# A vision-transformer kernel: GpSimd's order at the end of the experts stage, and per-tile loads from two queues after it

## What is computed

```python
topk_logits, topk_idx = jax.lax.top_k(router_logits, TOP_K)          # 2 of 8 experts for each row
x_sort = x_flat[token_ids_sort]                                      # rows sorted by expert
gate, up = jnp.split(jax.lax.ragged_dot(x_sort, moe_w13, group_sizes), [MOE_DIM], axis=-1)
out_dispatch = jax.lax.ragged_dot(silu(gate) * up, moe_w2, group_sizes)
out_flat = zeros.at[token_ids_sort].add(out_dispatch * w_sort[:, None])
...
h = h + out_flat
h = h + _L1_attn_ref(_layernorm(h, axis=-1), ...)                    # second layer's attention
```

## Time and profile before

| | us |
|---|---|
| three runs | 1926.74, 1930.16, 1930.44 (median 1930.16) |
| the profiled execution | 1924.54 |
| its span, first to last instruction | 1922.8 |
| experts stage in the profile | 725.6 to 973.8 |
| next stage in the profile | 974.4 to 1026.4 |

### The profile page before, as it was taken

The page is one execution under the profiler, slowest core; times in us unless marked ns, Lnnn a source line. Parts: engine busy times, 40 slices in busy tenths (PEclk is TensorE's granted clock), DMA queues, the critical chain, the costliest instruction groups (busy, mean ns, idle before and its releaser), DMA issues. The chain is left out here.

```text
span 1922.8 us, 35451 instructions
## 1 busy us (share of the span) xinstructions
PE 1474.6 (77%) x10564; PEld 872.9 (45%) x10565; DVE 1430.1 (74%) x4678; ACT 856.9 (45%) x2116; POOL 614.7 (32%) x1114
## 2 busy tenths in 40 slices
PE   7799898978888857999963786676667777676664
PEld 4222224544444444666642444554445445554553
DVE  4688886567777683111146999999999999899982
ACT  2366665215555522222234544454545554554432
POOL 3300000350000012333301445554555554555540
PEclk9799999988999978999976667667677766766767
DMA  6351230241212250111045012101030012200000
GB/s 167 101 167 50 60 91 1 66 127 39 64 52 50 109 217 21 44 39 41 32 145 141 10 28 55 48 7 29 9 98 12 9 29 51 80 2 13 1 1 13
DMA packets 72136, 111.45 MB, mean 58 GB/s; under 512 B 8684, under 2 KB 57766, under 8 KB 71212
## 3 DMA queue, kind: packets, MB, share of 16 engines
q1 hardware_dynamic: 68236, 101.18, 18.3%
q0 software_dynamic: 3744, 8.42, 1.4%
HBM read 73.86 MB, written 37.52 MB: 58 GB/s over the span
## 5 line engine op out<-in xcount | busy, mean ns | idle before, releaser
L1679 DVE MATCH_REPLACE8 top_left<-top_next,top_left 128x65 f32<-128x65 f32 (+15 forms) x768 | 321.7, 426 | 0.0
L1674 DVE MAX8 top_next<-top_left 128x8 f32<-128x65 f32 (+15 forms) x768 | 300.3, 431 | 0.0
L1134 POOL TENSOR_TENSOR top_e<-top_e,top_left 128x33 f32<-128x33 f32 (+3 forms) x254 | 188.7, 765 | 199.8 <-DVE top_left L1679 199.6
L1409 ACT ACTIVATE top_e<-top_ps_s,top_neg_max 128x129 f32<-128x129 f32 (+15 forms) x256 | 125.8, 492 | 184.7 <-POOL top_neg_max L1578 168.5
L743 DVE TENSOR_REDUCE tok_rowmax<-tok_ps_s 128x1 f32<-128x512 f32 x256 | 166.8, 688 | 28.6 <-PE tok_ps_s L585 25.8
L1252 PE MATMUL top_ps_pt<-ident,top_e 128*128 128x128 f32 x640 | 140.3, 349 | 24.9 <-issue 13.6
L2530 DVE TENSOR_TENSOR moe_hid<-moe_act_gate,moe_ps_h 128x512 f32<-128x512 f32 x39 | 26.8, 688 | 163.9 <-ACT moe_act_gate L2491 163.9
L743 DVE TENSOR_REDUCE rot_rowmax<-rot_ps_s 128x1 f32<-128x128 f32 (+3 forms) x256 | 115.7, 487 | 43.4 <-PE rot_ps_s L588 39.6
L716 ACT ACTIVATE tok_et<-tok_ps_st 128x1024 f32<-128x1024 f32 x128 | 124.1, 1021 | 50.6 <-PE tok_ps_st L619 50.6
L2430 PE MATMUL moe_ps_h<-moe_w,moe_rows_t 128*128 x312 | 142.3, 599 | 0.2 <-issue 0.2
L1421 ACT ACTIVATE top_prob_t<-top_ps_pt 128x128 f32<-128x128 f32 (+3 forms) x256 | 104.9, 432 | 78.4 <-PE top_ps_pt L1252 77.7
(11 more groups left out here) (384 smaller groups left out, 3221.6 us busy)
## 6 DMA issues: line engine op xcount, KB each, us to landing
moe_w<-in_moe_w SPq DMA_DIRECT2D x3, 4096.0 KB, 22.0
last_xs<-zeros SPq DMA_DIRECT2D x1, 5120.0 KB, 20.1
moe_got<-moe_ys SPq DMA_DIRECT2D x8, 512.0 KB, 6.4
top_vs<-v_by_position SPq DMA_DIRECT2D x16, 256.0 KB
k_parts<-rot_parts SPq DMA_DIRECT2D x16, 192.4 KB, 3.2
rot_ks<-k_parts SPq DMA_DIRECT2D x16, 192.4 KB
top_ks<-k_parts SPq DMA_DIRECT2D x16, 192.4 KB
q_parts<-tok_parts SPq DMA_DIRECT2D x16, 192.0 KB, 2.9
```

The costliest lines, as they stand in the source:

```text
L1134: eng.tensor_tensor(e[:, U % KEPT, 0:w], e[:, U % KEPT, 0:w], left[:, U % 4, 0:w], ALU.subtract).then_inc(prob_ok, 1)
L1409: act.activation(e[:, U % KEPT, 0:keys(U)], row(U), ACT.Exp, bias=neg_max[:, U % 4:U % 4 + 1]).then_inc(e_ok, 1)
L1674: dve.max(next8[:, U % 2, step // 2, :], left[:, U % 4, 0:keys(U)]).then_inc(pick, 1)
L1679: ins = dve.match_replace(left[:, U % 4, 0:w], next8[:, U % 2, step // 2 - 1, :], left[:, U % 4, 0:w], 0.0)
```

## The change

In `run_gated_experts`, GpSimd's list keeps its order for tiles 0 to 31. It then scatters tile 31 at once, and goes through a nest: if tile j exists, gather tile j + 2, free the result buffer of tile j, scatter tile j, and ask for tile j + 1 inside; else wait for the last two scatters. In `combine_project`, the first image's results are loaded by tiles of 128 KB, choice 0 from SyncE's queue and choice 1 from GpSimd's, each tile with semaphores of its own; the other three images as before. ScalarE waits for `eps` and takes an unused square root before its masks.

```diff
             used = used_tiles(pool)
             lag = 3
-            for i in range(2, TILES + lag):
-                if i < SURE_TILES + 2:
-                    regather_rows(i)
-                    free_y(i - 2)
-                elif i < TILES + 2:
-                    with pool.If(used > i - 2):
-                        if i < TILES:
-                            regather_rows(i)
-                        free_y(i - 2)
-                j = i - lag
-                if 0 <= j < SURE_TILES:
+            for i in range(2, SURE_TILES + 2):
+                regather_rows(i)
+                free_y(i - 2)
+                if i >= lag:
+                    scatter_y(i - lag)
+            scatter_y(SURE_TILES - 1)
+
+            def rest(j):
+                if j == TILES:
+                    last_landed(j)
+                    return
+                with pool.If(used > j):
+                    if j + 2 < TILES:
+                        regather_rows(j + 2)
+                    free_y(j)
                     scatter_y(j)
-                elif j >= 0:
-                    with pool.If(used > j):
-                        scatter_y(j)
-            for j in range(SURE_TILES - 2, TILES):
-                if j < SURE_TILES:
+                    rest(j + 1)
+                with pool.Else():
+                    last_landed(j)
+
+            def last_landed(end):
+                for j in (end - 2, end - 1):
                     pool.wait_ge(y_sent[j % 2], 16 * (j // 2 + 1))
-                else:
-                    with pool.If(used > j):
-                        pool.wait_ge(y_sent[j % 2], 16 * (j // 2 + 1))
+
+            rest(SURE_TILES)
...
-            for b in range(B):
+            for n in range(NQ):
+                sp.dma_start(got[:, 0, n, :], ys[n * P:(n + 1) * P, :]).then_inc(got_in[1 + n], 16)
+            for b in range(1, B):
                 for k in range(2):
                     at = k * ROWS + b * S
                     sp.dma_start(got[:, k, b * NQ:(b + 1) * NQ, :], ys[at:at + S, :].rearrange("(n p) d -> p n d", p=P)
-                                 ).then_inc(got_in[b + 1], 16)
+                                 ).then_inc(got_in[NQ + b], 16)
...
+        @block.gpsimd
+        def _(pool):
+            for n in range(NQ):
+                at = ROWS + n * P
+                pool.dma_start(got[:, 1, n, :], c.ys[came][at:at + P, :]).then_inc(got_too[n], 16)
...
-                pe.wait_ge(got_in[0 if i == 0 else 1 + (i - 1) // NQ], 16 * 2)
+                if 1 <= i <= NQ:
+                    pe.wait_ge(got_in[i], 16)
+                    pe.wait_ge(got_too[i - 1], 16)
+                else:
+                    pe.wait_ge(got_in[0 if i == 0 else NQ + (i - 1) // NQ], 16 * 2)
...
-                if i == 0:
-                    act.wait_ge(eps_ok, 1)
...
+            act.wait_ge(eps_ok, 1)
+            act.activation(root[:, :], eps[:, :], ACT.Sqrt)
             mask_keys(0)
```

More of the change, by code:

```diff
@@ L2977, in combine_project @@
         eps = c.sbuf(st, "mixed_eps", [P, 1], F32)
+        root = c.sbuf(st, "mixed_root", [P, 1], F32)
         xn = c.ctx
@@ L2991, in combine_project @@
         ps_s = c.psum(st, "mixed_ps_sum", [P, 2, S])
-        got_in = [c.sem(st, f"{came}_got_in{i}") for i in range(B + 1)]
+        got_in = [c.sem(st, f"{came}_got_in{i}") for i in range(NQ + B)]
+        got_too = [c.sem(st, f"{came}_got_too{i}") for i in range(NQ)]
         sum_mm = c.sem(st, "mixed_sum_mm")
```

## The result

The changed kernel is slower. The median of its 18 fast runs is 1939.0 us against 1929.77 us for the kernel before (20 runs), and the ratio is 1.0048 with a 95% interval of 1.0035 to 1.0061; two further executions took 2930.77 and 6184.63 us, for a reason that isn't known, and are left out. That is 9.3 us more (6.8 to 11.8). The forecast was 7.6 more, 1937.8 in all.

What follows compares the result with a forecast made beforehand. TensorE's own list was taken to pace the experts stage and GpSimd's drain to set its barrier. +8.9 (gathers) + 0.4 (jumps) - 1.7 (loads) = +7.6 us, so 1937.8 us on the median; forecast 1934 to 1941, range 1931.5 to 1942.

Steps and rivals of the forecast that it cites:

- The gathers: Experts stage, tiles 32 to 37: each gather comes one tile later and TensorE stalls before `turn_rows`, +8.9 us.
- 4.90 + L: Period of one late slot instead of 5.82 us; L is the time from gather start to its rows, 2.1 to 2.64.
- One sign: Expected in the profile: TensorE idle 1.3 to 1.6 us before `turn_rows`, waiting for the gather, six times.
- The questions: End of GpSimd's nest: six jumps of 0.16 us, 0.4 us lost; 0.3 gained if the compiler joins them.
- The drain: GpSimd's drain at the experts stage's end stays 6.44 us, since the same 78 indirect DMAs go ahead of it.
- the rival in which it shrinks: GpSimd's drain at the experts stage's barrier gives back up to 6.4 us, total +1.2, 1931.4 us; chance 0.1.
- The loads: Second stage, `combine_project`: tile loads and early root let TensorE start its first full tile sooner, 1.7 us gained.
- rise before the second tile: Second stage: without a gap TensorE's clock rises early, its 2.7 us for that tile are halved, gain 3.3 us.
- the case with a gain of only 1.2 us: Second stage: GpSimd issues no load until VectorE's bfloat16 copies end at 977.08, and data come at 979.5.
- The sum: Whole kernel: +8.9 + 0.4 - 1.7 = +7.6 us, bounds +3.5 and +10.9, 1937.8 us on the median.
- the way out: Experts stage, from the last scatter's landing to GpSimd's drain: 0.9 us of jumps instead of 0.5, +0.4 us.

Runs made afterwards that it cites:

- the drains between: GpSimd drains put between its indirect DMAs, on the changed kernel with the nest's scatter put back by one tile: 1920.84 us, ratio 0.9952.
- the two pairs: The kernel before and the changed kernel, each profiled twice without further edits; the second profiles took 1935.39 and 1932.99 us.

## Why the prediction was right

*The gathers.* Right in mechanism and size. The term was 8.9 us, with bounds of 7.1 and 10.3; the six slots cost 9.3. The period was put at 4.90 + L, with L = 2.4. The measured mean is 7.37, which by that formula makes L 2.47. Read off slot by slot, from the gather's start to `turn_rows`, L is 2.19 to 2.81 us, two of the six above the bound of 2.64. One sign came only in part: TensorE was to be idle 1.3 to 1.6 us before `turn_rows` six times. It was so four times, for 0.96 to 1.51 us, and in the other two slots the idle time stood behind register loads, which the prediction doesn't have. The sum hardly suffers, because the rows were awaited there too. Putting the order back removed all of it, with the nest still there, and sixteen more late gathers added 34.5 us. The clock stayed at 1.00 at 80% busy, as assumed.

*The questions.* The sign was wrong and the size small. I had six jumps at 0.16 us, 0.4 lost; the compiler joins them, and 0.3 us are gained, the other end of the range that was given.

*The drain.* It stayed at 6.44 us, as assumed, and the rival in which it shrinks did not happen. The reason in the prediction, that the same 78 DMAs precede it, agrees with what the drains between have shown.

*The loads.* 1.7 us were forecast; the profiles show 2.0 and 2.2 between the two pairs. The clock did not rise before the second tile, but during it, or right behind it in one of the seven profiles with these loads. Where it rose early in the tile the stage took 49.8 us, and where it rose late 50.4 or 50.5. GpSimd was quicker than I had put it: its first issue came at 982.91, 0.5 us after SyncE's, and the next ones 0.61 us apart, where I had 1.3 for both. It did not wait until VectorE's four copies were over, which was the case with a gain of only 1.2 us. The Trainium skill (SBUF — State Buffer, SBUF: two separate sides) says that a DMA issued from GpSimd is held while VectorE copies in a two-port mode. The trace doesn't speak against that for the single copy:

```profile
L3271 DVE COPY top_qs<-ident_bf x4: 690/694/805, 982.6 to 984.5; 32x2048 bf16<-32x2048 bf16 x4
```

The first of these copies, under way when GpSimd issued its first load, ended at 983.28. That load landed at 985.5, 2.6 us after its issue, where SyncE's first took 2.0, and the copy behind took 0.805 us instead of 0.69. A hand-over between two copies would look like this, but no run shows that it was one. What is shown is that holding up for the length of one copy costs nothing here, and that my case summed the four copies as if there were no gap between them.

*The sum.* Step by step it is +9.3 - 0.3 - 2.0 = +7.0 for the two stages, near the 7.6 of the forecast; part of that nearness is luck, as the gathers were put 0.4 too low, the way out 0.7 too high and the loads' gain 0.3 too low. The stages by their clears give +8.9 - 2.0 = +6.9. The measured 9.3 has 6.8 as its lower bound, so the two are just compatible. What lies between them is not explained by any step. The largest other difference, the attention stage's, comes out by chance.

## What to carry to other kernels

When a list is rewritten to make its control flow simpler, compare the order of the DMAs in it, not the branches: here a gather moved behind one more scatter cost 1.5 us per tile, because TensorE's in-order list left 1.04 us for it and it takes some 2.5. Here the branches stood in the shadow of a landing, and removing them gained 0.3 us at the most. Where a stage ends behind many DMAs of GpSimd, look at how long its last drain is, and try drains in its idle time earlier. And compare the stages of two profiles only after a look at the granted clock in each: two runs had a stage 1.7 us longer by a fall of the clock alone.

## What the runs showed of the hardware

GpSimd's drain is long behind many of its indirect DMAs, though the last has landed: 6.435 us behind 78 of them since the last drain, 0.287 us behind 2, which is some 0.08 us for each if it grows evenly. Behind the four loads still under way it ended about 0.2 us after the last had landed (990.7 against 990.4). What it does in that time isn't visible.

A stall of TensorE behind a wait has a second price, because its sequencer can't run ahead: register loads that were hidden come into the open. Three of them made 1.30 us of idle time in the changed kernel, five made 2.6 us with the late order from tile 16 on.

TensorE's clock fell to its lower level in some executions and not in others behind idle times of nearly the same length. After 2.62 and 2.59 us of idle time the granted clock over the next four microseconds was 0.60 and 0.65, after 2.58 us in the same profile it was 1.00. After the wait of 2.25 us in the second stage it fell in two of the eleven profiles (0.57), which cost 1.7 us each time.

Two DMA queues started the first image's tiles no sooner than one (4.5 and 4.4 us after SyncE's first load), because TensorE waited for no load in either case.
